# A ring of five slots instead of three for the queries' operand of the attention phases

## The reference

```
x = x + attention0(norm(x))   # 16 heads of 8, rotary, causal:  softmax(q k^T / sqrt(8)) v, projected
x = x + ffn0(norm(x))         # 128 -> 512, silu gate, two 512x512 layers with gelu, -> 128
x = x + attention1(norm(x))   # 16 heads of 8, latent q and kv of 64, rotary, biases, not causal
x = x + experts1(norm(x))     # 8 experts 128 -> 512 -> 128 with gelu, the best 2 of each row
```

## Time and profile before

| | |
|---|---|
| median of 3 runs | 1668.86 us (1667.9 to 1669.16) |
| the profiled execution | 1669.09 us, span 1667.4 us |
| mean granted clock of TensorE | 0.913 |
| TensorE matmuls busy | 1471.0 us (88%) |
| VectorE busy | 1165.0 us (70%) |
| ScalarE busy | 1045.8 us (63%) |
| GpSimd busy | 226.3 us (14%) |
| projection, layer 0 | from 16 to 52 us |
| attention, layer 0 | from 52 to 519 us |
| projection, layer 1 | from 714 to 778 us |
| attention, layer 1 | from 778 to 1484 us |
| issues of transfers of `Q` | 256, 32 KB each |

### The profile page before, as it was taken

One profiled execution on the slowest core, in us unless ns is written; L12 is line 12 of the kernel. 1 busy time (PEld: TensorE's weight loads), 2 busy tenths in 40 slices (PEclk: granted clock), 3 DMA queues, 4 the chain that ended last, 5 costly groups with the idle time before them and its releaser, 6 DMA issues. The chain is left out here.

```text
span 1667.4 us, 30716 instructions
## 1 busy us (share of the span) xinstructions
PE 1471.0 (88%) x11729; PEld 657.5 (39%) x11729; DVE 1165.0 (70%) x1556; ACT 1045.8 (63%) x1992; POOL 226.3 (14%) x314
## 2 busy tenths in 40 slices
PE   6768889999998999786799999999999999984774
PEld 3433343343334444332233333333333333343774
DVE  6756799999714011247999999999999998336223
ACT  2434568768885322223188888888888888861552
POOL 4122121211110000021000000000000000000674
PEclk9567899999999999965599999999999999995898
DMA  4200000000000000020000000000000000003455
GB/s 167 79 13 14 14 14 8 8 13 8 2 1 1 1 0 0 9 95 26 0 4 10 9 8 8 8 8 8 8 8 8 8 8 1 1 2 124 114 142 144
DMA packets 34286, 45.91 MB, mean 28 GB/s; under 512 B 6001, under 2 KB 18750, under 8 KB 33632
## 3 DMA queue, kind: packets, MB, share of 16 engines
q1 hardware_dynamic: 29535, 38.76, 7.7%
q0 software_dynamic: 2496, 4.21, 0.8%
q10 hardware_dynamic: 2112, 1.05, 0.2%
HBM read 36.06 MB, written 8.85 MB: 27 GB/s over the span
## 5 line engine op out<-in xcount | busy, mean ns | idle before, releaser
L628 DVE TENSOR_REDUCE maxp<-banks 128x2 f32<-128x1024 f32 (+3 forms) x800 | 941.7, 1199 | 121.1 <-PE banks L475 61.8
L611 ACT ACTIVATE probs<-banks 128x512 f32<-128x512 f32 x1568 | 842.3, 596 | 219.9 <-PE banks L501 172.8
L520 PE MATMUL banks<-probs,V 128*9 128x256 f32 (+3 forms) x6016 | 488.0, 399 | 3.7 <-POOL probs L575 3.0
L501 PE MATMUL banks<-Q,K 64*128 64x512 f32 (+3 forms) x1664 | 436.5, 485 | 8.1 <-ACT probs L611 4.7
L475 PE MATMUL banks<-K,Q 64*128 64x512 f32 (+3 forms) x1664 | 379.7, 437 | 61.1 <-DVE maxp L628 35.2
L501 PEld LDWEIGHTS banks<-Q,K 64*128 64x128 f32 x1664 | 181.0, 188 | 364.9 <-ACT probs L611 299.0
L475 PEld LDWEIGHTS banks<-K,Q 64*128 64x128 f32 x1664 | 181.3, 200 | 107.5 <-DVE maxp L628 73.6
L520 PEld LDWEIGHTS banks<-probs,V 128*9 128x9 f32 x6016 | 91.2, 88 | 252.7 <-ACT probs L611 194.8
L561 POOL CAST Q<-Q 32x512 fp32r<-32x512 f32 x64 | 38.8, 607 | 671.1 <-ACT Q L599 669.1
L808 PE MATMUL banks<-work,flex 128*128 128x512 f32 x256 | 110.5, 592 | 0.0
L575 POOL TENSOR_SCALAR_AFFINE_SELECT probs<-probs 128x256 f32<-128x256 f32 (+1 forms) x112 | 47.6, 439 | 363.7 <-ACT probs L611 363.0
(11 more groups left out here) (157 smaller groups left out, 918.8 us busy)
## 6 DMA issues: line engine op xcount, KB each, us to landing
ew<-in_down SPq DMA_DIRECT2D x39, 256.0 KB, 2.8
Q<-q_rows SPq DMA_DIRECT2D x256, 32.0 KB
tables<-in_tables SPq DMA_DIRECT2D x2, 2048.0 KB, 8.9
q_rows<-qb SPq DMA_DIRECT2D x8, 512.0 KB, 2.8
up_all<-in_up SPq DMA_DIRECT2D x1, 2064.0 KB, 12.3
flex<-in_h SPq DMA_DIRECT2D x2, 1024.0 KB, 7.9
x<-in_x SPq DMA_DIRECT2D x4, 256.0 KB, 3.9
xn_rows<-xn SPq DMA_DIRECT2D x1, 1024.0 KB, 6.8
```

Source lines behind the costliest of these rows:

```text
L501: mm = pe.matmul(ebank(e)[:, at:at + CW - low], k.K[rows, 2 * g + block, kt * P:(kt + 1) * P], k.Q[rows, n % 3, block, low:CW], start=True ...
L520: mm = pe.matmul(acc[32 * j:32 * j + HD + 1, low + a:low + z], k.V9[:, kt, g * HG + j, :], k.probs[:, tile, at + a:at + z], start=(s == 0) ...
L611: act.activation(k.probs[:, number % 8, :], ebank(e), ACT.Exp, scale=scale).then_inc(e_done, 1)
L628: dve.tensor_reduce(dst, src, AX.X, ALU.max).then_inc(m_done, 1)
```

## The change

`Q` has five slots instead of three, with a semaphore each. Every `n % 3` becomes `n % Q_RING`. The first five units' operands are loaded in the projection: those of units 0 to 3 behind the store of the first chunk, that of unit 4 behind the store of the second. In attention, the clear in unit n is for unit n + 4; it waits for the same scores as before (those of unit n - 1, whose slot it is). GpSimd waits for the clears so far before it spreads a shift. `norm_phase` does without `var_ready` and counts that step in `stats_step`.

```
+Q_RING = 5
...
-            dve.tensor_scalar(k.ve[:, :], k.mv[:, :, 1], EPS, None, ALU.add).then_inc(var_ready, 1)
+            dve.tensor_scalar(k.ve[:, :], k.mv[:, :, 1], EPS, None, ALU.add).then_inc(stats_step, 1)
             dve.wait_ge(std_ready, 1)
             dve.reciprocal(k.rstd[:, :], k.std[:, :]).then_inc(stats_step, 1)
-            dve.wait_ge(stats_step, 3)
+            dve.wait_ge(stats_step, 4)
...
-            act.wait_ge(var_ready, 1)
+            act.wait_ge(stats_step, 3)
...
-                if c == 0:
-                    sp.wait_ge(q_stored, 16)
+                mine = [n for n in range(Q_RING) if n // G == c]
+                if mine:
+                    sp.wait_ge(q_stored, 16 * (c + 1))
                     sp.wait_ge(q_cleared, 1)
-                    for n in range(3):
+                    for n in mine:
                         load_queries(sp, k, layer, n)
...
-            for n in range(3, NU):
-                sp.wait_ge(q_cleared, n - 2)
+            for n in range(Q_RING, NU):
+                sp.wait_ge(q_cleared, n - Q_RING + 1)
                 load_queries(sp, k, layer, n)
...
+                cleared = sum(1 for m in range(1, n) if m + Q_RING - 1 < NU)
+                if cleared:
+                    pool.wait_ge(q_cleared, cleared)
                 for half in (0, 1):
...
             def clear_queries(n):
-                m = n - 3
+                m = n - Q_RING
                 pool.wait_ge(e_done, e_number["scores", m, *halves[m][-1], 1] + 1)
-                pool.memset(k.Q[:, n % 3, :, :].bitcast(F32), 0.0).then_inc(q_cleared, 1)
+                pool.memset(k.Q[:, n % Q_RING, :, :].bitcast(F32), 0.0).then_inc(q_cleared, 1)
...
-                    if h == 1 and n >= 1 and n + 2 < NU:
-                        clear_queries(n + 2)
+                    if h == 1 and n >= 1 and n + Q_RING - 1 < NU:
+                        clear_queries(n + Q_RING - 1)
...
-        k.Q = sb("Q", [P, 3, 2, CW], F32R)
+        k.Q = sb("Q", [P, Q_RING, 2, CW], F32R)
```

More of the change, by code:

```diff
@@ L63, in norm_phase @@
         x_loaded, stats_step = [sem(f"x_loaded{c}") for c in range(C if first else 0)], sem("stats_step")
-        var_ready, std_ready, xn_ready = sem("var_ready"), sem("std_ready"), sem("xn_ready")
+        std_ready, xn_ready = sem("std_ready"), sem("xn_ready")
         turned, xnT_ready = sem("turned"), sem("xnT_ready")
@@ L157, in load_queries @@
             heads = k.q_rows[product // 2].rearrange("(h d) s -> d h s", d=HD)
-            sp.dma_start(k.Q[rows, n % 3, :, :].bitcast(F32), heads[:, HG * g + half:HG * (g + 1):2, c * CW:(c + 1) * CW]
-                         ).then_inc(k.q_loaded[n % 3], 16)
+            sp.dma_start(k.Q[rows, n % Q_RING, :, :].bitcast(F32), heads[:, HG * g + half:HG * (g + 1):2, c * CW:(c + 1) * CW]
+                         ).then_inc(k.q_loaded[n % Q_RING], 16)
 def project_phase(nc, k, layer):
@@ L467, in score_maxima @@
                 if i == 0:
-                    pe.wait_ge(k.q_loaded[n % 3], 16 * QUERY_COPIES * (n // 3 + 1 + layer * len(range(n % 3, NU, 3))))
+                    pe.wait_ge(k.q_loaded[n % Q_RING], 16 * QUERY_COPIES * (n // Q_RING + 1 + layer * len(range(n % Q_RING, NU, Q_RING))))
                 if m >= 2:
@@ L474, in score_maxima @@
                         out = mpair(m)[:, half, q * w:(q + 1) * w]
-                        mm = pe.matmul(out, k.Q[rows, n % 3, b, t * P:(t + 1) * P],
+                        mm = pe.matmul(out, k.Q[rows, n % Q_RING, b, t * P:(t + 1) * P],
                                        k.K[rows, 2 * g + b, a * CW:a * CW + w], start=True, stop=True)
@@ L501, in scores @@
                         mm = pe.matmul(ebank(e)[:, at:at + CW - low], k.K[rows, 2 * g + block, kt * P:(kt + 1) * P],
-                                       k.Q[rows, n % 3, block, low:CW], start=True, stop=True)
+                                       k.Q[rows, n % Q_RING, block, low:CW], start=True, stop=True)
                         if piece == len(jobs[x]) - 1:
@@ L559, in spread_shift @@
                     pool.wait_ge(masked, masks_done(n - 1, halves[n - 1][shift_at[n - 1]][0]))
+                cleared = sum(1 for m in range(1, n) if m + Q_RING - 1 < NU)
+                if cleared:
+                    pool.wait_ge(q_cleared, cleared)
                 for half in (0, 1):
-                    pool.tensor_copy(k.Q[shift_rows(half), n % 3, 1, :], k.Q[shift_rows(half), n % 3, 0, :]
+                    pool.tensor_copy(k.Q[shift_rows(half), n % Q_RING, 1, :], k.Q[shift_rows(half), n % Q_RING, 0, :]
                                      ).then_inc(spread_done, 1)
@@ L598, in take_shift @@
                 for half in (0, 1):
-                    copy = act.activation(k.Q[shift_rows(half), n % 3, 0, :], ebank(e)[shift_rows(half), :], ACT.Copy)
+                    copy = act.activation(k.Q[shift_rows(half), n % Q_RING, 0, :], ebank(e)[shift_rows(half), :], ACT.Copy)
                 copy.then_inc(e_done, 1)
@@ L1221, in build @@
         k.y_rows = nc.dram_tensor("y_rows", (2, S, D), F32, kind="Internal").ap()
-        k.q_loaded = [sem(f"q_loaded{slot}") for slot in range(3)]
+        k.q_loaded = [sem(f"q_loaded{slot}") for slot in range(Q_RING)]
         k.weights_loaded, k.tables_loaded = sem("weights_loaded"), sem("tables_loaded")
```

## The result

| | before | after |
|---|---|---|
| median of the runs, us | 1669.01 (1667.90 to 1670.15, 4 runs) | 1644.48 (1642.28 to 1645.90, 4 runs) |
| ratio, with its 95% interval | | 0.9854 (0.9839 to 0.9869) |
| the profiled execution, us | 1669.09 | 1645.46 |
| its span, us | 1667.4 | 1643.7 |
| mean granted clock of TensorE | 0.913 | 0.919 |

What follows compares the result with a forecast made beforehand. Late transfers of Q stop TensorE, and through it VectorE, in layer 0's attention. 20.6 us of VectorE's idle time plus 1.8, 0.5, 0.7, 2.8 and 1.5 of slow clock make 27.9: 1668.9 to 1641.0 us, range 1634 to 1650.

Steps and rivals of the forecast that it cites:

- The stops of Q: Layer 0's attention, units 1, 2, 3, 5, 6: all five waits for Q's transfers go, -20.60 us by VectorE's idle time.
- The lead: Loads of Q go out two units ahead, about 20 us, against the 4.42 us that a load takes.
- Unit 1, -1.8: Layer 0's attention, unit 1: the slow-clock stretch behind the first stop goes wholly, 1.8 us at most, all taken.
- Units 2 and 3, -0.5 and -0.7: Layer 0's attention: slow stretches partly go, from ranges of 0 to 1.3 and 0 to 2.8 us.
- Unit 4, the reference, 0: Layer 0's attention, unit 4: no stop, 19.18 us, the measure for unit 5; no gain forecast.
- Unit 5, -2.8, and unit 6, -1.5: Layer 0's attention: unit 5 should take unit 4's time, -2.8 us; unit 6 gains 1.5 of 0 to 2.8.
- What it adds: Larger clear, SyncE's longer projection queue, GpSimd's wait for clears, normalisation's semaphores, fewer clears and issues in attention: each costs 0.
- The rival in which the change ends slower through SyncE's queue: Projection's end moves to SyncE, its stores in series with forty loads: 1673 us or more, chance 0.02.
- the rival of no change: The wait moves within SyncE's queue, or VectorE's later work absorbs the gain: 1669 us, chance 0.02.
- the clock's term, 7.3 us: Layer 0's attention: gain from slow-clock stretches, 1.8, 0.5, 0.7, 2.8 and 1.5 us in units 1, 2, 3, 5, 6.
- two clock rivals: Layer 0's attention: clock low despite the stops going, 1648 us, chance 0.2; clock up throughout, 1636.8 us, chance 0.14.
- clock low all the same: Stops go, but TensorE drops to 1.2 GHz in units 2 and 3 or elsewhere; only 20.6 us won, 1648, chance 0.2.

Runs made afterwards that it cites:

- e1_late5: The changed kernel with five slots, but three units loaded in the projection and later loads as late as before, except the last two units'; 1670.52 us, 1.0021 of before.
- e2_ring4: The changed kernel with four slots for Q instead of five; 1645.03 us, 0.9868 of the kernel before.
- e10_warm_again: The changed kernel plus six filler matmuls before unit 2's shift wait and maxima doubled in half steps with five or more reductions; 1658.12 us, 0.9816 of before.
- e3_fill_stops: The kernel before, three slots, with extra matmuls of K by K ahead of the five waits for Q; 1664.09 us, 0.9972 of the kernel before.
- e7_before_again: The kernel before, unchanged, run once more for a second trace; one execution of 1685.46 us.
- e11_first2: The changed kernel with the maxima matmuls ahead of unit 0 issued twice, in both layers; 1672.88 us, 0.9902 of the kernel before.
- e12_first2_warm: The kernel of e10_warm_again with the maxima matmuls ahead of unit 0 also issued twice, in both layers; 1670.77 us, 0.9893 of the kernel before.

## Why the prediction was right, and where it was off

- **The stops of Q.** Right. All five are gone, 20.60 us by VectorE's idle time, and with the loads late again (e1_late5) the whole gain is gone. To count VectorE's idle time and not the 21.93 of TensorE's stops or the 24.3 of its weight loads was right too.
- **The lead.** Right, with room: one slot more would have done (e2_ring4).
- **Unit 1, -1.8.** Wrong. The argument was that TensorE comes in at 1.00 and has no burst, so the clock would stay up. It fell in the pause of 1.86 us for the shift, which had stood as 0.92 us behind the first stop in the earlier trace rows and got no term. e10_warm_again has extra matmuls in this pause, the clock stays, and unit 1 takes 10.02 us for 12.60, where the forecast came to 17.70 - 7.26 = 10.4. So the price of the slow stretch wasn't set too high; that it would go with the stop was wrong.
- **Units 2 and 3, -0.5 and -0.7.** Right as a judgement (0.4 and 1.1): in the changed kernel the clock falls there at 98 and 115 us without a stop, since TensorE has gaps of its own at VectorE's pace. The Trainium skill (TensorE: Matmul & The Clock Gate, Part 1) has idle gaps between bursts bring the clock down, and that agrees with the gaps of 1.31 and 0.71 us ahead of 98 us; what did not follow is that every slow stretch would go with its stop, by which the forecast would have been some 4 us lower.
- **Unit 4, the reference, 0.** It gained 0.5, since the clock of before was still low at its start, where two score matmuls take 0.79.
- **Unit 5, -2.8, and unit 6, -1.5.** Right for this pair of traces (3.3 and 2.2), and the stops counted under e3_fill_stops show the cause. But it was a reading of one execution: in e7_before_again the same unit lost only 0.8 us beyond VectorE's idle time (1.95 - 1.13).
- **What it adds.** All of it costs nothing, as forecast: the clear takes 4.36 (4.4 forecast) and ends in time, SyncE's last store goes out at 45.92, which with the 3.68 of the earlier trace rows is 49.6 (49.4 forecast), ahead of 52.40. The rival in which the change ends slower through SyncE's queue has nothing to stand on, and the rival of no change is refuted.
- **The sum.** The stretch with the stops gained 28.36 us in the profiled executions, for 27.9 forecast. That is in part luck: units 3 to 6 gained 2.1 us more than their terms, which made up for the 2.2 of unit 1. What was not forecast is that 4.7 us came back later, where the change does nothing: 0.4 at the start, 1.3 in the last units of layer 0's attention, 1.9 in its feed-forward part, the rest in small pieces. The feed-forward part takes 165.8 to 165.9, 167.8 or 168.9 us in the fourteen traces of all kernels, and the kernel before has both a 165.92 and a 168.92. It goes with how long the clock is low at its start (6.0, 10.2 and 13.4 us at the low level in a trace of each). So the profiled execution of before had this part at its shortest, and layer 0's attention at its longest: its clock losses were larger than its next trace shows.

So the step that failed is the size of the clock's term, 7.3 us. Against the medians it is 24.5 - 20.6 = 3.9. More traces agree with the smaller figure. From the shift's copies of unit 0 to those of unit 7, without VectorE's idle time in the five stops, the two traces of before take 128.15 and 125.85 us, and the three of the changed kernel 120.39, 124.35 and 126.16: the means are 3.4 us apart, an estimate from few traces on several chips. Of the two clock rivals neither came true: some stretches kept the clock and some lost it, and the result lies between the forecast and "clock low all the same" (1648), at 3.5 us from the one and as much from the other.

## What to carry to other kernels

Count what a late transfer costs by the idle time of the engine that sets the pace (here VectorE's five rows), not by the waits of the engine that it stops, and give the ring only the depth at which the load goes out one load's time ahead; the slot beyond that brought nothing. When a filler is to keep an engine busy, read from the trace how long it lasts: 28 matmuls took 3.44 us of a stop of 6.06. A clock loss that is read from one execution is one draw: look at a second trace of the same kernel before it goes into the sum, or leave it to the range. When a stop goes, look at the next short pause on the same engine, since here a wait of 1.86 us for the shift brought the clock down just as the stop had.

## What was not expected of the hardware

- The same stop of 1.7 to 1.8 us cost 1.95 us in one execution and 4.84 in another, on another chip, and 3.37 in e1_late5; whether the clock falls behind it isn't fixed.
- The clock also falls without a stop, in bursts at VectorE's pace: in after it is 1.00 at 94 to 98 us and 0.51 at 98 to 105, with no wait of TensorE over 1.31 us ahead of the fall.
- More work ahead of the first units did not raise it sooner: it is 0.50 until 81 us in e11_first2, and 1.00 from 78 us on in after.
- The experts' part takes 20 us longer on the second and third chips, in every kernel, while layer 1's attention takes 729.2 to 729.9 us on all three, e11_first2 and e12_first2_warm apart. Why is open.
